# A new order of VectorE, GpSimd and ScalarE in the first stage of a two-layer transformer kernel, with x loaded ahead of the projection slices

## The chip, the cores and the metric

The kernel runs on one core of a Trainium2 chip. The metric is the time of one execution on the device, in microseconds. Of the kernel before there are three timed runs and one profiled execution.

## The reference

x is 2 x 256 rows of 512, the context 2 x 512 rows of 512. `layernorm` has no gain or bias. Four residual steps follow each other:

```python
# 1: both operands fake-quantised to 8 bits, (clip(round(v / s + z), 0, 255) - z) * s
x = x + fq(layernorm(x)) @ fq(ctx)                              # per batch, 512 x 512
# 2: a gated feed-forward, 512 -> 1376 -> 512; in blocks of 32 along the contraction the
#    rows are rounded to fp6 and the weights to fp4, with a shared power of two per block
x = x + mx_ffn(layernorm(x), w_gate, w_up, w_down)
# 3: cross attention: 32 query heads over 8 key and value heads of 128, rotary, masked softmax
x = x + attention(layernorm(x), ctx, wq, wk, wv, wo, mask)
# 4: a gated feed-forward with plain weights, 512 -> 1376 -> 512
x = x + ffn(layernorm(x), gate_w, up_w, down_w)
```

## The kernel before

Every engine has a list of instructions of its own (`@block.sync`, `tensor`, `scalar`, `gpsimd`, `vector`), written out by hand. An engine takes its list in order; what it has to wait for is a count of a semaphore. One wait at the head of a list holds all that is behind it.

**The first stage** does three things beside each other. TensorE projects the context to keys and values of step 3, in units of 128 x 512 results: `("v", i, h)` is context tile i with half h of the value heads, `("k", i, b)` key head i of batch b, and `("l", b, n)` one of the three products of step 1's attention for batch b. `STEPS` (L41) lists the units of eight steps; each takes the next of four PSUM banks in turn (`ROTATE`, L63, `take`, L515), and so waits until the unit four places back has been read (`drained`, L290). The first four value units are done together, slice by slice of the contraction (`first_values`, L550): slice k needs `slice_load(k)` (L337), a quarter of the context's columns and of the value weights, 512 KB. `keep_busy` (L544) issues `WARM` matmuls of ones before that. Five key units come later (`LATE_KEYS`, L51), between the products of step 2 and the first scores.

ScalarE copies each unit out (`copy_values`, `copy_keys`, L879 and L886), SyncE stores it to memory, and the keys of head 0 are loaded again for rotation (`first_keys_load`, L356, six loads into the place of weight buffers; it waits for 14 counts of `mx_free`, which are the halves of chunks 0 to 6).

The fp4 weights of step 2 come in 9 chunks of 128 x 2048 (the last is 128 x 512). A chunk i goes through `mx_peaks` (L1412, VectorE: block maxima), `mx_exponents` (L1418, VectorE, into one of `NRAW` = 3 slots), `scale_in` (L1146, GpSimd: multiply by the inverse scale, two halves), `mx_lift` (L893, ScalarE: magnitude to PSUM, two halves; half h of chunk i waits for `mx_free` 2(i-1)+h+1), `mx_round` (L1424, VectorE: two instructions a half, the second counts `mx_free`), `mx_clip` (L1437, VectorE), `scale_out` (L1155, GpSimd: multiply back, two halves), and `chunk_turn` (L345, SyncE: a transposing DMA into `WT`). VectorE's loop over chunks (L1467) puts the peaks and exponents of chunk i+2 behind the rounding of chunk i; GpSimd's (L1189) `scale_in(i+2)` ahead of `scale_out(i)`.

Step 1 is woven in. VectorE normalises x (`layernorm(True)`, L1383), ScalarE scales and rounds it (`rows_scale`, `rows_round`, L901 and L907), VectorE clips it (`clip_rows`, L1385), ScalarE makes the bf16 rows (`rows_keep`, L912), SyncE turns them (`rows_turn`). The context goes the same way (`context_scale`, `context_round`, `clip_context`, `context_keep`). With `L0_AT` = 4 the product's rank-one part is written by ScalarE (`share`, L927), GpSimd adds it to X (`rows_add`, L1181), and VectorE adds the product (`attention0`, L1401), behind the rounding of chunks 4 and 5. Behind chunk 5 VectorE also rounds chunk 6, then takes the second layer norm and quantises its rows to fp6 (L1487 to L1494); GpSimd scales them (`rows_out`, L1164), SyncE turns them (`rows_turn_again`, L364, two DMAs), and TensorE begins the gate and up products (`gate_up_slice`, L594), which wait for that, for chunks 0 to 5 and for key unit (5, 0). The late key unit in front of them (L629) waits for all of `mx_free` up to chunk 7.

**Between the stages** come the gate, up and down products of step 2, the third layer norm, and then the attention's units U = -3 to 64 in five parallel lists (`unit`, L456, L778, L1062, L1223, L1571). Unit U takes in a query head (rotary: ScalarE swaps halves into `q_swp`, GpSimd multiplies by the sine, L1235, VectorE by the cosine, L1602, and adds, L1615), and a pair of head and batch in four parts j: `score` (L695), the row maximum (L1587), the exponential (`exponent`, L1042), the division (L1230), the transposes (`turn_probs`), the weighing and the projection. `score` n waits for n - 1 exponentials (L703).

## Time and profile before

| what | value |
|---|---|
| median of three runs | 683.6 us (683.54 to 683.84) |
| the profiled execution, timed on the device | 683.66 us |
| its span, first to last instruction | 681.9 us |
| TensorE busy | 659.7 us (97%) |
| VectorE busy | 518.0 us (76%) |
| ScalarE busy | 344.7 us (51%) |
| GpSimd busy | 471.5 us (69%) |

The span is 1.8 us shorter than the execution's own time, which also holds what lies around it. A busy share is an average over stages: what a change in one of them is worth must be read from that stage. In the rows PE is TensorE, DVE VectorE, ACT ScalarE, POOL GpSimd, and SPq SyncE's queue of DMA issues. Times of rows are in us from the start of the span. A record of an instruction is longer than its distance to the next one, since instructions overlap by a part of their length.

### The profile page before, as it was taken

What the parts mean: (1) busy time and instruction counts of PE and PEld (TensorE: products, weight loads), DVE (VectorE), ACT (ScalarE), POOL (GpSimd) and SP (SyncE); (2) the same over time, 40 slices, a digit from 0 to 9 for tenths busy, and PEclk for the clock granted to TensorE, in tenths of its full rate; (3) what the DMA queues carried; (4) which work ended last, traced back from release to release, by engine and by line L of the source; (5) the groups of instructions that cost most, each with busy time, mean ns of one, the idle gap of its engine ahead of it and who ended that gap; (6) DMA issues with size and microseconds to landing.
All of it is one profiled execution on the core that took longest, in us unless ns stands there. A gap on an engine that the chain in (4) does not pass through costs nothing.

```text
span 681.9 us, 10810 instructions
## 1 busy us (share of the span) xinstructions
PE 659.7 (97%) x2993; PEld 484.8 (71%) x2996; DVE 518.0 (76%) x1024; ACT 344.7 (51%) x665; POOL 471.5 (69%) x435
## 2 busy tenths in 40 slices
PE   9998999899799999999999999999999999899998
PEld 3443444446567888888888888888888877788886
DVE  5999797997788888888888888888888886621113
ACT  1795223424656656656656656556656663221111
POOL 0688937337598688688788788698688477066661
PEclk9999999999999999999999999999999999999999
DMA  8999678403222222222222121222224012012321
GB/s 315 390 343 248 200 195 185 155 1 123 92 79 77 63 78 78 62 79 75 62 79 75 62 84 70 62 77 77 62 78 138 17 32 83 10 48 94 110 73 62
DMA packets 61260, 73.15 MB, mean 107 GB/s; under 512 B 25265, under 2 KB 33585, under 8 KB 60209
## 3 DMA queue, kind: packets, MB, share of 16 engines
q1 hardware_dynamic: 61232, 72.83, 34.7%
q8 instruction: 12, 0.20, 0.1%
q14 instruction: 16, 0.12, 0.1%
HBM read 58.00 MB, written 9.44 MB: 99 GB/s over the span
## 4 chain that ended last, share of the span: by engine, by line
PE 73%; DVE 12%; POOL 7%; issue 4%; ACT 2%; DMA 1%; SPq 0%; POOLq 0%; DVEq 0%; ACTq 0%
PE ps L687 16%; PE ps L689 16%; PE ps L688 16%; PE ps L755 11%; PE ps L721 7%; PE ps L572 3%; PE ps L540 2%; POOL mx_raw L1153 2%; PE ps L608 2%; POOL mx_w L1162 2%; DVE mx_amax L1416 1%; DVE stats L1329 1%; DVE xhat L1358 1%; POOL prob L1230 1%; DMA X<-in_x 1%
## 5 line engine op out<-in xcount | busy, mean ns | idle before, releaser
L1230 POOL TENSOR_SCALAR prob<-prob,rinv 128x512 f32<-128x512 f32 x128 | 89.4, 698 | 72.4 <-DVE rinv L1594 72.3
L1049 ACT ACTIVATE prob<-ps,nmax 128x512 f32<-128x512 f32 x128 | 88.3, 690 | 97.8 <-DVE nmax L1587 95.3
L755 PE MATMUL ps<-xt,wq_sb 128*128 128x512 f32 x384 | 103.1, 393 | 0.1
L1060 ACT CAST pT<-ps 128x512 fp32r<-128x512 f32 x128 | 75.1, 587 | 51.4 <-PE ps L721 50.4
L1587 DVE CUSTOM_DVE_ANT_0 ps<-ps,mask_sb 128x512 f32<-128x512 f32 x128 | 87.8, 686 | 5.1 <-PE ps L689 5.0
L1610 DVE TENSOR_TENSOR pT<-ps,pT 128x512 fp32r<-128x512 f32 x128 | 86.2, 674 | 3.0 <-ACT pT L1060 2.0
L755 PEld LDWEIGHTS ps<-xt,wq_sb 128*128 128x128 f32 x384 | 71.8, 188 | 17.2 <-issue 1.0
L721 PE MATMUL ps<-idf,prob 128*128 128x128 f32 x512 | 76.7, 272 | 0.4 <-POOL prob L1230 0.3
L721 PEld LDWEIGHTS ps<-idf,prob 128*128 128x128 f32 x512 | 63.8, 142 | 17.3 <-POOL prob L1230 1.6
L687 PE MATMUL ps<-pT,vt 128*128 128x512 f32 x128 | 61.2, 478 | 0.9 <-DVE pT L1610 0.9
L540 PE MATMUL ps<-ctxT,wk_sb 128*128 128x512 f32 x128 | 57.7, 594 | 0.0
L687 PE MATMUL ps<-kt,qt 128*128 128x512 f32 x128 | 50.8, 397 | 4.0 <-ACT prob L1049 3.5
L687 PE MATMUL ps<-wo_sb,oT 128*128 128x512 f32 x128 | 50.5, 394 | 2.0 <-DVE oT L1657 1.5
L1665 DVE SCALAR_TENSOR_TENSOR int<-ps,sc,silu 128x512 f32<-128x512 f32 x11 | 8.3, 750 | 57.6 <-PE ps L689 57.6
L1235 POOL TENSOR_TENSOR q_swp<-q_swp,ropeQ 128x512 f32<-128x512 f32 x32 | 47.5, 1484 | 6.1 <-ACT q_swp L1070 6.1
L689 PE MATMUL ps<-pT,vt 128*128 128x512 f32 x128 | 50.8, 397 | 0.0
L688 PE MATMUL ps<-pT,vt 128*128 128x512 f32 x128 | 50.3, 393 | 0.0
L1207 POOL TENSOR_TENSOR wo_sb<-wo_raw,wo_sb 128x512 fp32r<-128x512 f32 x32 | 48.4, 1512 | 2.7
L689 PE MATMUL ps<-kt,qt 128*128 128x512 f32 x128 | 50.1, 392 | 0.0
L688 PE MATMUL ps<-wo_sb,oT 128*128 128x512 f32 x128 | 50.0, 391 | 0.0
L689 PE MATMUL ps<-wo_sb,oT 128*128 128x512 f32 x128 | 50.0, 391 | 0.0
L688 PE MATMUL ps<-kt,qt 128*128 128x512 f32 x128 | 49.9, 390 | 0.0
(177 smaller groups left out, 1542.3 us busy)
## 6 DMA issues: line engine op xcount, KB each, us to landing
mx_raw<-in_mxw SPq DMA_DIRECT2D x8, 1024.0 KB, 6.9
wq_raw<-in_wq SPq DMA_DIRECT2D x32, 256.0 KB, 3.2
wo_raw<-in_wo SPq DMA_DIRECT2D x32, 256.0 KB, 2.6
v_scr<-v_st SPq DMA_DIRECT2D x16, 256.0 KB, 3.9
k_scr<-k_st SPq DMA_DIRECT2D x16, 256.0 KB, 3.4
kr<-k_scr SPq DMA_DIRECT2D x16, 256.0 KB, 2.8
kr_swp<-k_scr SPq DMA_DIRECT2D x32, 128.0 KB, 3.3
vr<-v_scr SPq DMA_DIRECT2D x16, 256.0 KB, 3.4
```

The costliest lines, as they stand in the source:

```text
L540: last = mm(bank(n), wk_sb[:, i % 2, k], ctxT[:, k, b * CTX:(b + 1) * CTX], start=(k == 0), stop=(k == KD - 1))
L687: mm(out_ap, left[0], right[0], start=first, stop=False)
L688: mm(out_ap, left[0], right[1], start=False, stop=False)
L689: return mm(out_ap, left[1], right[0], start=False, stop=final)
L721: last = nc.tensor.transpose(bank(2 + i % 2)[:, k * P:(k + 1) * P], prob[:, i, k * P:(k + 1) * P], idf[:])
L755: last = mm(query_bank(H), wq_sb[:, par, l, k], xt[:, r, k], start=(n == 0), stop=(n == 11))
L1049: nc.scalar.activation(prob[:, j], bank(j % 2), ACT.Exp, bias=nmax[:, j:j + 1], scale=-1.0, accum_out=rsum[:, j:j + 1]).then_inc(exps, 1)
L1060: copy(pT[:, v % 2, 0, :, i * P:(i + 1) * P], bank(2 + i % 2).rearrange("p (k c) -> p k c", k=4)).then_inc(ph_ready, 1)
L1207: tt(low, raw, high.bitcast(F32), ALU.subtract).then_inc(l_done, 1)
L1230: nc.gpsimd.tensor_scalar(prob[:, i], prob[:, i], rinv[:, i:i + 1], 1.0, ALU.mult, ALU.mult).then_inc(probs, 1)
L1587: nc.vector.tensor_tensor_reduce(out=bank(j % 2), in0=bank(j % 2), in1=mask_sb[:, 2 * (u % 2) + j % 2], scale=-1.0, scalar=BIG, op0=ALU.ad ...
L1610: tt(pT[:, v % 2, 1, :, i * P:(i + 1) * P], bank(2 + i % 2).rearrange("p (k c) -> p k c", k=4), pT[:, v % 2, 0, :, i * P:(i + 1) * P].bitc ...
```

## The change

- SyncE loads x's four row tiles first, then slice 0, weight chunk 0 and slices 1 to 3. Before, slices 0 and 1 came first, then x, slice 2, chunk 0, slice 3. All that follows stays as it was.
- `WARM` is 12 instead of 8.
- The exponents get a fourth slot (`NEXP`), so that VectorE's exponents of a chunk wait for one `scale_out` less.
- The clip of x's rows goes from VectorE (behind the peaks of chunk 2) to GpSimd (behind `scale_in(1)`).
- VectorE adds the first attention's products before GpSimd adds the rank-one part: `attention0` stands behind the exponents of chunks 5 and 6 (i = 3 and 4) and no longer waits for `l0_added`; `rows_add` waits for `l0_read` and stands ahead of `scale_in(6)` and `scale_in(7)`.
- The rounding of chunk 6 stands behind the second layer norm and the fp6 quantising, not ahead of them.
- ScalarE does `share(0)` ahead of `context_keep(1)`.
- SyncE's stores of k(4,1) and the units after it stand behind `chunk_turn(5)`, most of them behind the turning of the rows.
- At the start of the attention: the last late key unit is split over U = -2 and U = -1, GpSimd's sine for U = -2 goes between the two halves of a weight split, and the first row maximum and exponential are issued earlier.

The diff, cut to its core (the body of `row_max` is the old one, and `query_sine` is the old wait and multiplication in a function):

```diff
 NRAW = 3
+NEXP = 4
...
-WARM = 8
+WARM = 12
...
-            mx_e = sb("mx_e", [P, NRAW, CH // BLK], F32, a)
+            mx_e = sb("mx_e", [P, NEXP, CH // BLK], F32, a)
...
             sp.dma_start(sc[:], scalars).then_inc(sc_in, 16)
-            slice_load(0)
-            slice_load(1)
             for t in range(NT):
                 sp.dma_start(X[:, t], x[t * P:(t + 1) * P]).then_inc(x_in[t], 16)
+            slice_load(0)
+            mx_load(0)
+            slice_load(1)
             slice_load(2)
-            mx_load(0)
             slice_load(3)
...
             first_keys_load()
-            stores(STEPS[5][1] + STEPS[6][0])
             chunk_turn(5)
-            stores(STEPS[6][1])
+            stores(STEPS[5][1] + STEPS[6][0][:1])
             rows_turn_again(0)
             rows_turn_again(1)
-            stores(STEPS[7][0])
+            stores(STEPS[6][0][1:] + STEPS[6][1] + STEPS[7][0])
...
-                    if isinstance(U, int) and U == -1 and j == 3:
-                        late_keys(4, range(1, 4))
+                    if isinstance(U, int) and U in (-2, -1) and j == 3:
+                        late_keys(4, range(1, 2) if U == -2 else range(2, 4))
...
             copy_keys(2, 1)
+            share(0)
             context_keep(1)
-            share(0)
...
                 for j in range(4):
+                    if isinstance(U, int) and U == 0 and j == 0:
+                        exponent(0, 0, 0)
...
-                    exponent(U, u, j)
+                    if not (isinstance(U, int) and U == 0 and j == 0):
+                        exponent(U, u, j)
...
                     pool.wait_ge(l0_shared, t + 1)
+                    pool.wait_ge(l0_read, t + 1)
                     tt(X[:, t], X[:, t], xhat[:, t], ALU.add).then_inc(l0_added, 1)

             scale_in(0)
             scale_in(1)
+            pool.wait_ge(q1_rounded, 1)
+            rows = xhat[:].rearrange("p t d -> p (t d)")
+            ts(rows, rows, ROUND, ROUND + 255.0, ALU.max, ALU.min).then_inc(q1_clipped, 1)

             for i in range(NFULL):
+                if i in (L0_AT, L0_AT + 1):
+                    rows_add(i - L0_AT)
                 if i + 2 <= NFULL:
                     scale_in(i + 2)
-                if i in (L0_AT - 1, L0_AT):
-                    rows_add(i - L0_AT + 1)
                 scale_out(i)
...
-            def split(high, low, raw, h_done, l_done, count):
+            def split(high, low, raw, h_done, l_done, count, between=None):
                 pool.sem_inc(pool_past_wait, 1)
                 nc.gpsimd.tensor_scalar(high, raw, 1.0, 1.0, ALU.mult, ALU.mult).then_inc(h_done, 1)
+                if between:
+                    between()
                 pool.wait_ge(h_done, count)
                 tt(low, raw, high.bitcast(F32), ALU.subtract).then_inc(l_done, 1)
...
-                    if isinstance(U, int) and U in (-2, -1) and j == 0:
-                        query_split(U, u, g)
-                    if j == 0 and within(U + 2, NH):
-                        pool.wait_ge(q_swapped, U + 3)
-                        tt(q_swp[:].rearrange("p (b c) -> p b c", b=BATCH), q_swp[:].rearrange("p (b c) -> p b c", b=BATCH),
+                    if isinstance(U, int) and U == -2 and j == 0:
+                        query_split(U, u, g, lambda: query_sine(-2))
+                    elif j == 0 and within(U + 2, NH):
+                        if isinstance(U, int) and U == -1:
+                            query_split(U, u, g)
+                        query_sine(U)
...
-            def clip_rows():
...
                     dve.wait_ge(l0_sums, 2 * b + t % 2 + b + 2)
-                    dve.wait_ge(l0_added, t + 1)
                     stt(X[:, t], bank(rotating(("l", b, t % 2 + 1))), sx[:, 4:5], X[:, t], ALU.mult, ALU.add).then_inc(l0_read, 1)
...
-                after(dve, mx_ready, 2 * (i - NRAW + 1))
+                after(dve, mx_ready, 2 * (i - NEXP + 1))
...
             for i in range(NFULL):
-                if i != L0_AT + 2:
-                    mx_round(i, 0)
-                    mx_round(i, 1)
+                mx_round(i, 0)
+                mx_round(i, 1)
                 if i + 2 <= NFULL:
                     mx_peaks(i + 2)
-                if i in (L0_AT, L0_AT + 1):
-                    attention0(i - L0_AT)
-                if i == 0:
-                    clip_rows()
...
                 mx_clip(i)
                 if i + 2 <= NFULL:
                     mx_exponents(i + 2)
+                if i in (L0_AT - 1, L0_AT):
+                    attention0(i - L0_AT + 1)
                 if i == L0_AT + 1:
-                    mx_round(i + 1, 0)
-                    mx_round(i + 1, 1)
-                    dve.wait_ge(l0_read, NT)
+                    dve.wait_ge(l0_added, NT)
                     layernorm(False)
...
-                    if within(U, NUNIT):
...
+                    if within(U, NUNIT) and not (isinstance(U, int) and U == 0 and j == 0):
+                        row_max(U, u, j)
...
                         tt(q_cos[:], q_cos[:], q_swp[:], ALU.add).then_inc(q_roped, 1)
+                    if isinstance(U, int) and U == -1 and j == 2:
+                        row_max(0, 0, 0)
```

## Rows read from the trace of the kernel before

**Rows 1.** Busy time by stretch: us; busy (instructions) per engine, clock, DMA share, GB/s

```profile
0.00:111.00 111.00, 104.56 (x251) 44.63 (x253) 98.11 (x132) 54.58 (x67) 70.08 (x51) 1.00 0.90 273
...
200.00:570.00 370.00, 368.64 (x1849) 304.23 (x1848) 313.63 (x684) 229.52 (x495) 294.17 (x291) 1.00 0.23 70
```

**Rows 2.** Timeline of TensorE: start, duration, line, tiles, count [idle before <-releaser]

```profile
1.01 3.59 PE L548 MATMUL ps<-ones 128*128 128x512 bf16 x8 [1.01 <-POOL ones L1138]
4.93 14.25 PE L558 MATMUL ps<-wv_sb,ctxT 128*128 128x512 f32 x32 [0.32 <-DMA wv_sb<-in_wv]
...
26.83 7.11 PE L572 MATMUL ps<-wv_sb,ctxT 128*128 128x512 f32 x16 [0.79 <-DMA wv_sb<-in_wv]
...
78.12 7.13 PE L572 MATMUL ps<-wv_sb,ctxT 128*128 128x512 f32 x16 [1.36 <-DVE X L1406]
...
111.04 9.96 PE L608 MATMUL ps<-WT,q1T 128*128 128x512 bf16 x48
```

**Rows 3.** Timeline of VectorE, the first weight chunks

```profile
22.04 1.21 DVE L1432 SCALAR_TENSOR_TENSOR mx_raw<-ps,mx_raw 128x1024 f32<-128x1024 bf16 x1
...
29.00 1.22 DVE L1387 TENSOR_SCALAR xhat<-xhat 128x2048 f32<-128x2048 f32 x1
...
30.84 1.22 DVE L1432 SCALAR_TENSOR_TENSOR mx_raw<-ps,mx_raw 128x1024 f32<-128x1024 bf16 x1
```

**Rows 4.** Timeline of GpSimd, 59 to 105 us

```profile
59.45 0.24 POOL L1149 TENSOR_SCALAR mx_r<-mx_e 128x64 int32<-128x64 int32 x1 [1.88 <-DVE mx_e L1422]
...
70.52 0.24 POOL L1149 TENSOR_SCALAR mx_r<-mx_e 128x64 int32<-128x64 int32 x1 [0.32 <-DVE mx_e L1422]
...
85.65 3.78 POOL L1162 TENSOR_TENSOR mx_w<-mx_q,mx_e 128x1024 bf16<-128x1024 bf16 x2
100.07 4.23 POOL L1168 TENSOR_TENSOR q<-f6c,f_e 128x1024 bf16<-128x1024 bf16 x2 [10.63 <-DVE f6c L1460]
```

**Rows 5.** Timeline of VectorE, second layer norm and fp6

```profile
86.19 2.46 DVE L1329 BATCH_NORM_STATS2 stats<-X 128x6 f32<-128x512 f32 x4
...
89.10 0.36 DVE L1344 TENSOR_SCALAR var_eps<-meanvar 128x4 f32<-128x4 f32 x1
...
99.90 0.68 DVE L1416 TENSOR_REDUCE mx_amax<-mx_raw 128x16 f32<-128x512 f32 x1
...
102.45 1.88 DVE L1422 TENSOR_SCALAR mx_e<-mx_amax 128x16 uint32<-128x16 uint32 x1
```

**Rows 6.** Timeline of ScalarE, 89 to 93 us

```profile
89.21 1.98 ACT L899 ACTIVATE ps<-mx_raw 128x1024 f32<-128x1024 f32 x2
92.16 0.59 ACT L884 COPY k_st<-ps 128x512 f32<-128x512 f32 x1 [0.97 <-PE ps L540]
```

**Rows 7.** Timeline of SyncE's issues; last, median us from issue at 103.56 to landing

```profile
92.12 0.63 SPq L360 DMA_DIRECT2D kr<-k_scr  x1
...
100.06 2.76 SPq L349 DMA_TRANSPOSE WT<-mx_w  x1
...
103.56 3.03 SPq L367 DMA_TRANSPOSE q1T<-q  x2
...
q1T<-q SPq DMA_TRANSPOSE x1, 4.0
```

**Rows 8.** SyncE's issues of x and chunk 0, and from issue to landing of each

```profile
3.09 1.85 SPq L374 DMA_DIRECT2D X<-in_x  x4
...
DMA to landing us min/median/max: 5.1/5.4/5.7
...
6.10 0.71 SPq L312 DMA_DIRECT2D mx_raw<-in_mxw  x1
...
mx_raw<-in_mxw SPq DMA_DIRECT2D x1, 1024.0 KB, 7.9
```

**Rows 9.** Timelines of ScalarE and TensorE at the first scores

```profile
175.02 0.69 ACT L1049 ACTIVATE prob<-ps,nmax 128x512 f32<-128x512 f32 x1
...
175.95 0.47 PE L687 MATMUL ps<-kt,qt 128*128 128x512 f32 x1 [1.91 <-ACT prob L1049]
```

More of the change, by code:

```diff
@@ L1148, in scale_in @@
                 pool.wait_ge(mx_expo, i + 1)
-                ts(mx_r[:, p, 0:m].bitcast(I32), mx_e[:, p, 0:m].bitcast(I32), -1.0, -(2.0 ** 24), ALU.mult, ALU.add).then_inc(mx_scale, 1)
+                ts(mx_r[:, p, 0:m].bitcast(I32), mx_e[:, i % NEXP, 0:m].bitcast(I32), -1.0, -(2.0 ** 24), ALU.mult, ALU.add).then_inc(mx_scale, 1)
                 pool.wait_ge(mx_scale, i + 1)
@@ L1158, in scale_out @@
                     pool.wait_ge(WT_in[i - 2], 16)
-                p, e = i % 2, i % NRAW
+                p, e = i % 2, i % NEXP
                 for cols in halves(i):
@@ L1214, in _, with query_sine, query_split @@
             split(wq_sb[:, 0, 0], wq_sb[:, 0, 1], wq_raw[:, 0], wqh_ready, wq_split, 1)
-            def query_split(U, u, g):
+            def query_sine(U):
+                pool.wait_ge(q_swapped, U + 3)
+                tt(q_swp[:].rearrange("p (b c) -> p b c", b=BATCH), q_swp[:].rearrange("p (b c) -> p b c", b=BATCH),
+                   ropeQ[:, 1].unsqueeze(1).to_broadcast([P, BATCH, SEQ]), ALU.mult).then_inc(q_sined, 1)
+            def query_split(U, u, g, between=None):
                 H, par = U + 4, u % 2
@@ L1220, in query_split @@
                     after(pool, q_sums, H - 1)
-                    split(wq_sb[:, par, 0], wq_sb[:, par, 1], wq_raw[:, par], wqh_ready, wq_split, H + 1)
+                    split(wq_sb[:, par, 0], wq_sb[:, par, 1], wq_raw[:, par], wqh_ready, wq_split, H + 1, between)
             def unit(U, u, g):
@@ L1383, in quantise_rows @@
                 layernorm(True)
-            def clip_rows():
-                dve.wait_ge(q1_rounded, 1)
-                ts(rows(xhat[:]), rows(xhat[:]), ROUND, ROUND + 255.0, ALU.max, ALU.min).then_inc(q1_clipped, 1)
             def clip_context(b):
@@ L1418, in mx_exponents @@
             def mx_exponents(i):
-                p, m = i % NRAW, width(i) // BLK
-                after(dve, mx_ready, 2 * (i - NRAW + 1))
+                p, m = i % NEXP, width(i) // BLK
+                after(dve, mx_ready, 2 * (i - NEXP + 1))
                 dve.wait_ge(mx_peak, i + 1)
@@ L1569, in _, with row_max @@
             dve.wait_ge(mask_in, 16)
+            def row_max(U, u, j):
+                n = 4 * U + j
+                dve.wait_ge(scores, n + 1)
+                dve.sem_inc(dve_past_wait, 1)
+                nc.vector.tensor_tensor_reduce(out=bank(j % 2), in0=bank(j % 2), in1=mask_sb[:, 2 * (u % 2) + j % 2],
+                                               scale=-1.0, scalar=BIG, op0=ALU.add, op1=ALU.min,
+                                               accum_out=nmax[:, j:j + 1]).then_inc(rowmax, 1)
             def unit(U, u, g):
@@ L1581, in unit @@
                         tt(oT[:, u % 2, 1], bank(4 + u % 2), oT[:, u % 2, 0].bitcast(F32), ALU.subtract).then_inc(o_split, 1)
-                    if within(U, NUNIT):
-                        n = 4 * U + j
-                        dve.wait_ge(scores, n + 1)
-                        dve.sem_inc(dve_past_wait, 1)
-                        nc.vector.tensor_tensor_reduce(out=bank(j % 2), in0=bank(j % 2), in1=mask_sb[:, 2 * (u % 2) + j % 2],
-                                                       scale=-1.0, scalar=BIG, op0=ALU.add, op1=ALU.min,
-                                                       accum_out=nmax[:, j:j + 1]).then_inc(rowmax, 1)
+                    if within(U, NUNIT) and not (isinstance(U, int) and U == 0 and j == 0):
+                        row_max(U, u, j)
                     V, v, i = (U, u, j - 1) if j else (U - 1, (u - 1) % 4, 3)
```

1 line of the change is left out of this document (removed).

## The prediction

> **What bounds the kernel now.** I read the busy time by stretch first. From 200 to 570 us TensorE is busy 368.64 of 370.00 us, so a shift of its work ahead of that passes to the end one for one, and what matters is when the first stage lets go. There, up to 111 us, TensorE has 104.56 us of work and VectorE 98.11: neither has much slack [rows 1]. TensorE's timeline then shows its projections, in records 0.43 us apart, starting at 4.93 and reaching the gate and up products of the first feed-forward at 111.04 without a wait. On the way it stood still for a load (0.79 us) and three times for the first attention's banks, 1.50, 1.36 and, in the row shown, 1.36 [rows 2].
>
> VectorE rounds weight chunk 0 from 22.04, in four instructions of 1.2 us like the one shown, so 4.8 us a chunk, and chunk 1 from 30.84; the rows' clip stands between them [rows 3]. GpSimd runs from 59.45 to 89.43, stopping only twice for 0.32 us, one of them shown; its end there is 85.65 + 3.78 [rows 4]. VectorE begins the second layer norm at 86.19. The four-wide operation at 89.10 lasts 0.36, to 89.46, the end of GpSimd's work, and the layer norm and its fp6 quantising are over at 99.90 [rows 5]. At 102.45 a small operation that needs 0.2 us takes 1.88 and ends at 104.33, with GpSimd's pair of 100.07 to 104.30 [rows 4, 5]. So GpSimd holds VectorE's operations of these kinds for a whole instruction.
>
> ScalarE lifts chunk 7 at 89.21 and copies k(4,1) at 92.16 [rows 6]. SyncE issues the first keys' six loads from 92.12, about 0.62 us each, the transpose of chunk 5 at 100.06 and the rows' two at 103.56; the first of those two lands 4.0 us later, at 107.6, in time for 111.04 [rows 7].
>
> **The start.** x now goes first, slice 0 second, chunk 0 third. The queue lands in order, so I read places off by megabytes. The second row tile was the bytes up to 1.5 MB: issued near 3.56, landed at 8.8; the fourth (2.0 MB) 4.52 + 5.7 = 10.2; chunk 0 (3.5 MB) 6.10 + 7.9 = 14.0 [rows 8]. Now slice 0 ends at 1.5 MB, 8.8; slice 1 at 3.0 MB, about 12.7; the later two by 14.0 and 15.3. A slice is eight records, 3.4 us: 8.9 to 12.3, a 0.5 us wait, 12.8 to 23.1. Before, this pass ended at 19.0: +4.1. The 0.79 us wait at 26.83 is then past: +3.3 [rows 2].
>
> Twelve warm matmuls instead of eight cost 4 x 0.45 = 1.8 us at most and end near 6.4, in front of 8.8: nothing.
>
> The layer norm of x is over some 3 us earlier, but ScalarE copies v(0,0) and v(1,0) ahead of lift 0, and they wait for the late pass. Unit 0 is summed at 20.9, unit 1 at 21.7; a copy (0.6) and a lift (1.0) [rows 6] give rounding at 23.4 instead of 22.04: +1.3. GpSimd takes the rows' clip off VectorE, -1.1 [rows 3]: chunk 1 is rounded at +0.2. GpSimd does it between scale_in(1) and scale_in(2), which waits for chunk 2's exponents until 31; at most it costs twice its nearest row's 1.9 us for 1024 columns of two inputs, 3.8 [rows 4], at least VectorE's 1.2, and I take 2.5. Either fits behind rows_round at 26.2. Were it not to fit, one or two us of rows_keep would be late, which nothing needs before the rows' first transpose.
>
> **The middle.** The copies, lifts and context steps in ScalarE's queue move by up to 3 us with TensorE, still ahead of their readers. Sharing before context_keep(1) frees the bank for v(4,1) in time. TensorE, 3.3 late, finds the attention's banks drained: its waits (4.2) go, so by itself it would reach 111.04 at 110.1, -0.9. On VectorE attention0 goes behind exponents and in front of rounding 4 and 5; rows_add waits for l0_read, and VectorE no longer for l0_added. The fourth exponent slot removes two waits of VectorE for scale_out. GpSimd is the chain here: from 59.7 it has the same instructions, with its adds in front of the scaling, and so ends again at about 89.5 [rows 4].
>
> The second layer norm no longer has rounding of chunk 6 in front of it: it can start at 86.2 - 4.8 + 0.3 = 81.7. It then runs beside scale_in(7) and scale_out(5). Statistics pass. The first small operation, at 84.6, waits to about 85.9, the next to 87.8, the next to 89.7. The other eight steps (0.2 each) and the normalising (1.9) come after, so the layer norm ends where it did, and fp6 at about 100.0 [rows 5]. That stall of about 4.6 us is what cancels the early start. The Trainium skill (SBUF — State Buffer, section SBUF: two separate sides) calls the shared pair an exclusive lock for a whole instruction, taken by any VectorE operation with two SBUF inputs too. No row shows the tiny two-input ones; with the rule the sum is mine, without it that of the second rival.
>
> **What hangs on chunk 6.** Its rounding is now behind fp6: 100.0 to 104.8, where it ended at 86.19. Three queues wait for it.
> - SyncE: first_keys_load waits for mx_free 14, that rounding, and all behind it waits too. 104.8 + 3.7 (six loads) + 2.8 (chunk 5) + 1.1 (two stores) = 112.4, the issue of the rows' transpose; + 4.0 = 116.4 [rows 7]. Moving two stores behind it saves about 1.1 and is in this sum.
> - ScalarE: lift(7,0) and lift(7,1) wait for the same, and k(4,1)'s copy is behind them: 104.8 + 1.0 + 0.6 = 106.4 [rows 6].
> - TensorE: v(7,1) needs k(4,1)'s bank. It is idle from 100.5 to 106.4, then has 3.4 + 3.4 + 1.7 (v(7,1), k(5,0), half a late key) = 115.0. The late key's wait for chunk 7's rounding, 110.8, is inside.
>
> So the gate product starts at 116.4 instead of 111.04: +5.4. From there to 200 us chains of VectorE and TensorE follow one another from that product on, and shift with it.
>
> **The late edits.** k(7,1)'s four matmuls are the same work at two places; the sine between the halves of one split comes 1.3 us earlier, but TensorE is busy without a gap up to 174.0, the first score included, so that buys nothing. The first maximum and exponential go ahead of q_swp. TensorE waited 1.91 at 175.95 for that exponential; at best this goes. But q_swp is now behind the exponential's 0.9 us, and the next maximum is behind q_swp on VectorE: at worst +0.9 [rows 9]. Score 3, which needs the second exponential, then waits instead. I take 0, since the wait moves by one score.
>
> **Sum.** -0.9 never shows, +5.4 replaces it. The profiled execution took 683.66 (span 681.9); 683.66 + 5.4 = 689.06. It is 0.06 above the median 683.6, so 689.0.
>
> **Rivals.**
> - The clock falls (15%). The eight bf16 matmuls at the start took 0.45 us each, the 1.2 GHz level, against 0.21 in the 48 at 111.04, 2.4 GHz; the granted column reads 1.00 at both. TensorE had been idle before the eight [rows 2]. No pause over 1.91 us is in the rows used. If 5.9 us idle drops it, some 3.6 us run at half pace and 1.8 are lost: 115.0 becomes 116.8, the forecast +0.4, 689.4. If the pause from 6.4 to 8.9 does too, the head of every queue is 1.8 late: 691.2. The Trainium skill (TensorE: Matmul & The Clock Gate, Part 1) has the clock return to half after idling; by that rule the first of these is likely.
> - Only some small operations are held (15%). Two are (89.10 and its like), the two-input ones not: fp6 ends near 98.2, everything 1.8 less: 687.2.
> - None is held (10%). 81.7 + 13.7 = 95.4, 4.6 less: +0.8, 684.4. Against it speak 0.36 at 89.10 and 1.88 at 102.45.
> - Not slower (18%): chunk 6 is done in time. SyncE needs 11.6 us from its rounding to the landing, so from an end at 99.4 downward nothing is lost, and at 98.5 TensorE's own 110.1 rules. It takes free small operations and x's order costing no 1.3 us. Then -0.9, 682.7; with the late wait of 1.91 gone too, 680.8. For it: the rows' order does bring x 3 us forward, and two waits of VectorE go.
> - The forecast has the other 42%.
>
> The measurement can tell about 0.2%, 1.4 us. Faster than 682.2 is 12% (the fourth rival with the late gain), within is 13% (its rest and part of the third), slower 75%. The range: 682.6 takes in most of the fourth, 691.5 the clock twice; outside are some 12% below and 5% above.
>
> **What would show it.** Right: first values at 8.9 and out of the last slice near 23; rounding 0 at 23.4; layer norm starting near 81.7 with small operations of 1 to 2 us; chunk 6 rounded after 104; SyncE's key loads after that; TensorE idle some 6 us before its last value product; the gate product at 116. Wrong: fp6 over by 96, key loads before 100, the gate product before 111, or a gap of 1.9 us at the scores that simply goes.

## The result and the profile after

The changed kernel takes 695.05 us in the median of four runs (693.14 to 695.89), the kernel before 683.72 (683.54 to 684.21): a ratio of 1.0161, with a 95% interval from 1.0138 to 1.0184. That is 11.3 us slower. The forecast was 689.0, slower by 5.4, and 691.5 was the top of its range: the direction was right, the size wrong by 6 us.

| what | before | after |
|---|---|---|
| profiled execution | 683.66 us | 695.89 us |
| its span | 681.9 us | 694.0 us |
| TensorE busy | 659.7 us | 666.7 us |
| VectorE busy | 518.0 us | 525.3 us |
| start of the gate product | 111.04 us | 121.25 us |

The span grew by 12.1 us, of which 10.2 lie ahead of the gate product. This is busy time by stretch in the changed kernel: us; busy (instructions) of TensorE, its weight loads, VectorE, ScalarE and GpSimd; granted clock; DMA share; GB/s.

```profile
0.00:111.00 111.00, 99.98 (x238) 43.24 (x239) 98.16 (x125) 51.78 (x63) 73.42 (x51) 0.96 0.81 246
8.60:24.00 15.40, 15.39 (x32) 6.76 (x33) 7.91 (x15) 4.08 (x4) 7.47 (x6) 0.89 1.03 399
...
109.50:116.00 6.50, 6.46 (x8) 2.71 (x9) 4.33 (x4) 1.45 (x3) 4.79 (x3) 0.53 1.01 231
...
200.00:570.00 370.00, 367.83 (x1837) 302.60 (x1837) 314.74 (x685) 231.47 (x497) 294.58 (x288) 1.00 0.22 71
```

Against [rows 1] the late stretch is as full as it was. In the first 111 us TensorE has less work done, and its granted clock is no longer 1.00: it is 0.89 over the first values and 0.53, all but the lower level of 1.2 GHz, from 109.5 to 116. TensorE's timeline shows the same, beside [rows 2]:

```profile
0.99 5.30 PE L548 MATMUL ps<-ones 128*128 128x512 bf16 x12 [0.99 <-POOL ones L1141]
8.61 15.67 PE L558 MATMUL ps<-wv_sb,ctxT 128*128 128x512 f32 x32 [2.31 <-DMA wv_sb<-in_wv]
...
91.71 10.46 PE L572 MATMUL ps<-wv_sb,ctxT 128*128 128x512 f32 x24
109.54 6.72 PE L572 MATMUL ps<-wv_sb,ctxT 128*128 128x512 f32 x8 [7.37 <-ACT k_st L884]
116.09 5.31 PE L540 MATMUL ps<-ctxT,wk_sb 128*128 128x512 f32 x12
121.25 9.96 PE L608 MATMUL ps<-WT,q1T 128*128 128x512 bf16 x48
```

The 24 value matmuls at 91.71 take 10.46 us, 0.43 each. The eight of the same kind at 109.54, behind a pause of 7.37 us, take 6.72, twice as long each. The waits for the first attention's banks, 4.2 us before, are gone, as forecast, and nothing came of it.

VectorE's timeline, beside [rows 3] and [rows 5]:

```profile
24.14 1.23 DVE L1441 SCALAR_TENSOR_TENSOR mx_raw<-ps,mx_raw 128x1024 f32<-128x1024 bf16 x1 [3.76 <-ACT ps L899]
...
31.13 3.55 DVE L1449 TENSOR_SCALAR mx_q<-mx_q 128x2048 bf16<-128x2048 bf16 x1
...
34.69 1.21 DVE L1441 SCALAR_TENSOR_TENSOR mx_raw<-ps,mx_raw 128x1024 f32<-128x1024 bf16 x1
...
84.99 2.48 DVE L1343 BATCH_NORM_STATS2 stats<-X 128x6 f32<-128x512 f32 x4
87.50 0.38 DVE L1349 BATCH_NORM_AGGREGATE meanvar<-stats 128x2 f32<-128x6 f32 x4
87.92 1.31 DVE L1358 TENSOR_SCALAR var_eps<-meanvar 128x4 f32<-128x4 f32 x1
89.26 1.83 DVE L1361 TENSOR_SCALAR rstd<-var_eps 128x4 int32<-128x4 int32 x1
91.13 1.83 DVE L1368 SCALAR_TENSOR_TENSOR newton<-rstd 128x4 f32<-128x4 f32 x1
92.99 0.16 DVE L1369 TENSOR_TENSOR newton<-newton,var_eps 128x4 f32<-128x4 f32 x1
...
102.99 1.22 DVE L1441 SCALAR_TENSOR_TENSOR mx_raw<-ps,mx_raw 128x1024 f32<-128x1024 bf16 x1
```

Chunk 0 is rounded from 24.14, 2.1 us later than before; chunk 1 from 34.69, 3.85 later. Between them stands a clip of chunk 0 that takes 3.55 us instead of 0.69. From there the delay is carried: layer norm at 84.99, then exactly three small operations held (1.31, 1.83, 1.83, against 0.16 for the next; GpSimd works without a stop from 85.42 to 92.94, and the third ends at 92.96), fp6 over and chunk 6's rounding begun at 102.99. What held the clip stands in GpSimd's timeline, the one instruction that moved there:

```profile
27.06 7.07 POOL L1194 TENSOR_SCALAR xhat<-xhat 128x2048 f32<-128x2048 f32 x1 [2.47 <-ACT xhat L910]
```

It runs to 34.13, and the clip of chunk 0 ends 0.55 us behind it. On ScalarE's queue the lift of chunk 7 waits for chunk 6's rounding, 16.49 us up to 105.56 for its first half, and the copy that TensorE's last value product waits for stands behind the second half, at 108.91:

```profile
108.91 0.58 ACT L884 COPY k_st<-ps 128x512 f32<-128x512 f32 x1
```

The same rounding holds SyncE's queue, beside [rows 7]; the rows' transpose lands 4.3 us after its issue, at 120.3:

```profile
107.88 0.34 SPq L361 DMA_DIRECT2D kr<-k_scr  x1
...
111.29 3.46 SPq L350 DMA_TRANSPOSE WT<-mx_w  x1
114.80 0.58 SPq L323 DMA_DIRECT2D k_scr<-k_st  x1
115.43 0.42 SPq L328 DMA_DIRECT2D v_scr<-v_st  x1
115.96 2.87 SPq L368 DMA_TRANSPOSE q1T<-q  x2
```

Behind the gate product another 1.9 us are lost. TensorE's timeline at the first scores, beside [rows 9], and GpSimd's:

```profile
178.29 3.02 PE L755 MATMUL ps<-xt,wq_sb 128*128 128x512 f32 x12 [0.74 <-POOL wq_sb L1216]
185.63 0.47 PE L687 MATMUL ps<-kt,qt 128*128 128x512 f32 x1 [0.28 <-ACT prob L1049]
188.94 0.50 PE L687 MATMUL ps<-kt,qt 128*128 128x512 f32 x1 [1.46 <-ACT prob L1049]
```

```profile
175.28 1.29 POOL L1227 TENSOR_TENSOR q_swp<-q_swp,ropeQ 128x512 f32<-128x512 f32 x1 [0.49 <-ACT q_swp L1072]
176.52 1.72 POOL L1216 TENSOR_TENSOR wq_sb<-wq_raw,wq_sb 128x512 fp32r<-128x512 f32 x1
```

The wait of 1.91 us shrank to 0.28, but 1.46 follows at the next score, and the split's low half now comes behind the sine, so that TensorE waits 0.74 for it. In the kernel before the low half starts 0.70 us after the start of its high half (163.92), here 2.35 after it (174.17). GpSimd's timeline before:

```profile
164.62 1.29 POOL L1207 TENSOR_TENSOR wq_sb<-wq_raw,wq_sb 128x512 fp32r<-128x512 f32 x1
```

### The profile page after: what moved, and what is told of

Read it like the earlier page. It is cut to its first block, busy times and chain, and to the rows that moved or that the text cites. A ratio compares the mean times of both kernels' runs of the same rounds, so it can differ in the third digit from the quotient of the medians.

```text
span 694.0 us, 10820 instructions
## 1 busy us (share of the span) xinstructions
PE 666.7 (96%) x3000; PEld 487.2 (70%) x3000; DVE 525.3 (76%) x1023; ACT 345.5 (50%) x665; POOL 479.6 (69%) x436
## 4 chain that ended last, share of the span: by engine, by line
PE 66%; DVE 19%; issue 7%; POOL 4%; ACT 3%; DMA 1%; SPq 0%; DVEq 0%; ACTq 0%; POOLq 0%
PE ps L687 14%; PE ps L689 14%; PE ps L688 14%; PE ps L755 10%; PE ps L721 6%; DVE mx_raw L1441 2%; PE ps L558 2%; PE ps L608 2%; DVE mx_amax L1425 2%; PE ps L540 2%; DVE ps L1579 1%; PE ps L572 1%; DVE stats L1343 1%; DVE xhat L1372 1%; DVE mx_q L1449 1%
## 5 line engine op out<-in xcount | busy, mean ns | idle before, releaser
L687 PE MATMUL ps<-kt,qt 128*128 128x512 f32 x128 | 51.0, 399 | 3.3 <-ACT prob L1049 2.7
L572 PE MATMUL ps<-wv_sb,ctxT 128*128 128x512 f32 x96 | 45.5, 627 | 7.4 <-ACT k_st L884 7.4
L689 PE MATMUL ps<-kt,qt 128*128 128x512 f32 x128 | 50.2, 392 | 0.0
```

The costliest lines, as they stand in the source:

```text
L572: last = mm(bank(n), ctxT[:, k, i * P:(i + 1) * P], wv_sb[:, k, h * 512:(h + 1) * 512], start=(k == 0), stop=(k == KD - 1))
L687: mm(out_ap, left[0], right[0], start=first, stop=False)
L689: return mm(out_ap, left[1], right[0], start=False, stop=final)
```

## The experiments

The theory after reading the trace: the chain that was forecast (layer norm held, chunk 6 late, SyncE's queue) is right, and GpSimd's clip, TensorE's clock and the late edits add what is missing. The rivals: the clip fits and costs nothing; the loads are what costs; the pace of TensorE has nothing to do with its pauses; the late edits are free.

### The rows' clip back on VectorE

```diff
-            pool.wait_ge(q1_rounded, 1)
-            ts(rows, rows, ROUND, ROUND + 255.0, ALU.max, ALU.min)
...
+                if i == 0:
+                    clip_rows()
```

> The changed kernel, with one part undone: the rows' clip is on VectorE again, behind the peaks of chunk 2, instead of on GpSimd. Theory (the clip takes GpSimd 7.07 us, keeps scale_in(2) and so VectorE's clip of chunk 0 waiting, and makes rounding of chunk 1 start at 34.69 us): VectorE's 3.55 us clip of chunk 0 goes back to about 0.6, the rows' clip costs about 1.1, rounding of chunk 1 starts near 33, and the gate product and the end come about 1.7 us earlier, 693.4 us, ratio to the kernel before 1.014. Rival (the clip fits beside other work, as predicted): rounding of chunk 1 may move, the gate product stays at 121.3 and the time at 695.1, 1.0165.

693.62 us, 1.0151 (1.0133 to 1.0169). VectorE's timeline:

```profile
30.96 1.22 DVE L1398 TENSOR_SCALAR xhat<-xhat 128x2048 f32<-128x2048 f32 x1
32.09 0.69 DVE L1450 TENSOR_SCALAR mx_q<-mx_q 128x2048 bf16<-128x2048 bf16 x1
...
32.80 1.22 DVE L1442 SCALAR_TENSOR_TENSOR mx_raw<-ps,mx_raw 128x1024 f32<-128x1024 bf16 x1
```

Chunk 0's clip takes 0.69 again and chunk 1 is rounded 1.9 us earlier. The medians differ by 1.4 us where 1.7 was expected, and the intervals of the two kernels overlap, so that the time alone does not decide. The trace shows the hold gone. In this profiled execution the gate product even starts 3.1 us earlier, at 118.15; 1.2 of that is its last value product, which took 5.53 us instead of 6.72.

### A product in place of the clip

```diff
-            ts(rows, rows, ROUND, ROUND + 255.0, ALU.max, ALU.min)
+            ts(rows, rows, 1.0, 1.0, ALU.mult, ALU.mult)
```

> The changed kernel, with GpSimd's 2048-column instruction a product by 1.0 and 1.0 instead of a maximum and a minimum, so x's rows are not clipped; same operands, same place, same waits. Theory (it is the kind of operation that is dear: GpSimd's products by two constants take 0.6 to 0.7 us for 512 columns): this one takes 2.4 to 2.8 us instead of 7.07, VectorE's clip of chunk 0 is not held beyond 1.3 us, rounding of chunk 1 starts near 32 instead of 34.69, time about 692.0 to 692.5 us, ratio 1.012 to 1.013. Rival (any one-input instruction over 2048 float32 columns takes 7 us on GpSimd, 3.45 ns a column): 7.07 us, 34.7, 695.

The rows are not clipped in this kernel. 690.47 us, 1.0111 (1.0089 to 1.0133). GpSimd's timeline, then VectorE's:

```profile
25.41 1.90 POOL L1194 TENSOR_SCALAR xhat<-xhat 128x2048 f32<-128x2048 f32 x1 [1.31 <-ACT xhat L910]
```

```profile
29.48 0.68 DVE L1449 TENSOR_SCALAR mx_q<-mx_q 128x2048 bf16<-128x2048 bf16 x1
...
30.18 1.22 DVE L1441 SCALAR_TENSOR_TENSOR mx_raw<-ps,mx_raw 128x1024 f32<-128x1024 bf16 x1
```

The same bytes in the same place cost 1.90 us as a product and 7.07 as a maximum and a minimum. So it is the kind of operation, and the rival with 3.45 ns for every one-input column falls; which of the two, the maximum or the minimum, is dear was not separated. The Trainium skill (GPSIMD Engine Reference, 4.1 Engine selection) calls GpSimd roughly line-rate for one input; the product agrees, 0.93 ns a column, the maximum and minimum do not, 3.45 ns. The gain is 4.6 us by the medians, 3.4 by the ratios, where 2.5 to 3 was expected. In the trace the hold of 2.9 us is gone; another part is TensorE's clock, which did not fall at the start of this profiled execution: chunk 0 is rounded at 22.50 instead of 24.14. Runs at the same mean granted clock tell the two apart: three of this kernel at 0.995 took 690.1 to 690.6, the one run of the changed kernel at 0.995 took 693.14, 2.8 us more; this kernel's fourth, at 0.989, took 693.4 against 695.6 and 695.89 of the changed kernel at 0.990. So the clip is worth some 2.2 to 2.8 us, from one run or two on each side. In this profiled execution the gate product starts at 115.58 where the prediction had 116.4, so the clip and the clock at the start make up all of the first stage's miss. The last value product still took 5.56 us there, behind a pause of 5.13.

### Chunk 6 rounded ahead of the layer norm again

```diff
                 if i == L0_AT + 1:
+                    mx_round(i + 1, 0)
+                    mx_round(i + 1, 1)
                     dve.wait_ge(l0_added, NT)
```

> The changed kernel, with one part undone: chunk 6 is rounded ahead of the second layer norm and its fp6 again, as before the change; the order of rows_add and l0_read stays the new one. Theory (the layer norm gains nothing from its early start, and the rounding put behind it holds up SyncE's key loads, ScalarE's lifts and TensorE's last value product): the layer norm ends at about the same time, near 103 to 104; the key loads go out near 92 instead of 105; TensorE has no pause of 7 us before its last value product and shows no stretch at half the granted clock there; the gate product starts near 114.5 instead of 121.3; time about 688.3 us, ratio 1.0067. Rival (the layer norm's early start is worth what the late rounding costs): gate product at 119 or later, time 693 or more, ratio 1.0135 or more.

689.46 us, 1.0092 (1.0069 to 1.0115), 5.6 us under the changed kernel by the medians, 4.7 by the ratios. TensorE's timeline:

```profile
110.89 2.41 PE L540 MATMUL ps<-ctxT,wk_sb 128*128 128x512 f32 x4 [3.70 <-DVE mx_q L1444]
113.09 11.23 PE L608 MATMUL ps<-WT,q1T 128*128 128x512 bf16 x48
```

Its fp6 is over at 101.55. This profiled execution runs 1.8 us ahead from the start, since the clock did not fall there; without that lead the changed kernel's 102.99 would be 101.15. So 4.8 us of rounding ahead of the layer norm delay its end by 0.4: its early start was worth almost nothing, and the rival falls. SyncE loads the keys at 89.91 instead of 107.88, and the pause of 7.37 us before the last value product is gone. One of 3.70 us takes its place, for chunk 7's rounding, and the gate product behind it takes 11.23 us instead of 9.96: the clock again.

### The old loads

```diff
-WARM = 12
+WARM = 8
...
+            slice_load(0)
+            slice_load(1)
             for t in range(NT):
                 sp.dma_start(X[:, t], x[t * P:(t + 1) * P]).then_inc(x_in[t], 16)
```

> The changed kernel, with one part undone: the old order of the first loads (slices 0 and 1, x, slice 2, chunk 0, slice 3, chunk 1) and eight instead of twelve warm matmuls. Theory (GpSimd's long clip, 26 to 33 us, rules the start whatever the loads do): the first values start near 5, TensorE is ahead of the others by up to 4 us more and gives that back before its last value product; rounding of chunk 1 starts near 34.0 instead of 34.69; time about 0.7 us less, 694.4, ratio 1.0155. Rival (the late loads are the cost: 3.3 us on TensorE and 1.3 on VectorE): 691 to 692 us, ratio 1.011 to 1.012.

694.22 us, 1.015 (1.0133 to 1.0167). Chunk 0 is rounded at 21.71, 2.4 us earlier, but chunk 1 at 33.59, only 1.1 earlier: GpSimd's clip runs from 25.95 to 33.02 and takes the rest. The time is 0.8 us less, within the intervals, and the rival, loads as the main cost, falls for this kernel, where the clip hides what they cost.

### TensorE kept busy in the pause

```diff
-                for k in range(KD):
+                for _ in range(3 if (i, h) == (7, 0) else 1):
+                    for k in range(KD):
```

> The changed kernel, with the first half-width value product of the last row tile (24 us of the first stage's end) computed three times instead of once, so that TensorE works through most of its pause ahead of the last value product; 16 matmuls are extra work, the output is the same. Theory (the 7.4 us of idling halve the pace of the following 8 matmuls): these take 0.43 us each instead of 0.85, 3.4 us in all instead of 6.7; the gate product is then set by the transpose of the rows, which lands near 120.2, so it starts at 120.0 to 120.3 instead of 121.3; time about 1.1 us less, 694.0, ratio 1.015. Rival (idling isn't what halves the pace): the eight matmuls still take 6.7 us, and the time is the same or up to 3 us more.

TensorE's timeline:

```profile
109.98 3.70 PE L573 MATMUL ps<-wv_sb,ctxT 128*128 128x512 f32 x8 [0.52 <-ACT k_st L885]
...
120.43 9.95 PE L609 MATMUL ps<-WT,q1T 128*128 128x512 bf16 x48 [1.60 <-DMA q1T<-q]
```

The eight matmuls take 3.70 us instead of 6.72, with the pause down to 0.52, so the pause was the cause of their pace. The gate product now waits 1.60 us for the rows' transpose, as expected. The time did not fall, though: 695.97 us, 1.0169 (1.0148 to 1.019). The start was 0.4 us later in the profiled execution, and of the 0.8 us won at the gate product nothing is left 39 us later: TensorE then waits 0.33, 1.15 and 0.90 us for VectorE between the gated slices, where it waited 0.56 and 1.15. The time of this run was missed by 2 us.

Then the same with SyncE's key loads behind the rows' transposes:

```diff
-            first_keys_load()
             chunk_turn(5)
...
             rows_turn_again(1)
+            first_keys_load()
```

> The changed kernel with v(7,0) computed three times, and SyncE's six key loads moved behind the rows' transposes. Theory (with TensorE kept at the full clock, the gate product waited 1.60 us for the transpose of the rows, and this stood behind the key loads, which wait for chunk 6's late rounding): the transposes go out near 105.5 instead of 116 us, land by 110, the wait of 1.60 us goes, and the gate product starts near 118.8 instead of 120.4, on TensorE's own work; time 694.0 to 694.4, ratio 1.0145 to 1.015. Rival (another wait stands right behind): gate product at 120 or later, 695.5 or more.

693.75 us, 1.0147 (1.0129 to 1.0165), an interval that overlaps the changed kernel's, and in TensorE's timeline no wait at the gate product:

```profile
109.68 3.70 PE L573 MATMUL ps<-wv_sb,ctxT 128*128 128x512 f32 x8 [0.20 <-ACT k_st L885]
...
118.37 9.95 PE L609 MATMUL ps<-WT,q1T 128*128 128x512 bf16 x48
```

So two chains met at the gate product within a microsecond: SyncE's, through the key loads, and TensorE's, through the half-paced product. Either alone hides the other: the gate product came 0.8 us earlier with the first step and 2.9 with both.

### Warm matmuls up to the first slice

```diff
-WARM = 12
+WARM = 24
```

> The changed kernel with 24 warm matmuls at the start instead of 12, so that TensorE works up to the landing of slice 0. Theory (the pause of 2.3 us behind the warm matmuls makes the first value product run at half pace for about 3.4 us, in some executions and not in others, which costs the head of every queue 1.6 us and spreads the times over 2.7 us): the 32 value matmuls all stand 0.43 us apart and end near 22.3 instead of 24.1 us, rounding of chunk 0 starts near 22.5, the time is 693.3 us with a spread under 1 us, ratio 1.0138. Rival (the pause is no cause): as the changed kernel, 693.1 to 695.9, median 695.

693.94 us, 1.0141 (1.0126 to 1.0157), spread 1.2 us. TensorE's timeline:

```profile
8.41 3.67 PE L558 MATMUL ps<-wv_sb,ctxT 128*128 128x512 f32 x8 [0.25 <-DMA wv_sb<-in_wv]
12.51 10.54 PE L558 MATMUL ps<-wv_sb,ctxT 128*128 128x512 f32 x24 [0.42 <-DMA wv_sb<-in_wv]
```

All 32 stand 0.43 us apart, and chunk 1 is rounded at 33.46 instead of 34.69. The median gains 1.1 us of the 1.7 expected; the intervals overlap, and it is the trace that shows the cause.

### The late edits, together and apart

The first run puts all of them on the kernel before, as the change's diff has them.

> The kernel before, with the late edits alone: the first maximum and exponential ahead of the sum for the second query, the sine between the two halves of one weight split, k(7,1)'s four matmuls at two places. The first stage is that of before. Theory (the wait of 1.91 us comes back as other waits, and the split's low half is late for TensorE): from the gate product to the first score 61.2 instead of 60.15 us, from there to the end 511.5 instead of 510.7; time 683.8 + 1.9 = 685.7 us, ratio 1.0028. Rival (worth nothing, as predicted): 683.8 us, within 0.3.

685.2 us, 1.0018 (1.0009 to 1.0027), and 1.0 us more from gate product to end. The next two take GpSimd's edit alone and the first maximum and exponential alone.

```diff
+                        query_split(U, u, g, lambda: query_sine(-2))
```

```diff
+                    if isinstance(U, int) and U == -1 and j == 2:
+                        row_max(0, 0, 0)
...
+                    if isinstance(U, int) and U == 0 and j == 0:
+                        exponent(0, 0, 0)
```

> The kernel before, with GpSimd's late edit alone: the sine product between the high and the low half of one query weight's split. Theory: the low half is ready 1.7 us later, TensorE waits about 0.7 us for it in front of the twelve matmuls at 178 us of the changed kernel, and the first score is as much later; time 683.8 + 0.7 = 684.5 us, ratio 1.001. Rival 1: all of the 1.07 us ahead of the first score come from it, 684.9. Rival 2: the sine's early end gives the wait back by the scores, 683.8.

> The kernel before, with one late edit alone: VectorE's first maximum and ScalarE's first exponential ahead of the steps for the second query; the sine and k(7,1) as before. Theory (the late edits cost 1.1 us together, and the sine's place nothing, so the maximum's place costs it): the wait of 1.91 us for the exponential shrinks to 0.3, and waits of 1.5, 0.5 and 0.3 us follow that the kernel before has not; time about 1.1 us over the kernel before, 685.0 us, ratio 1.0016. Rival (the split of k(7,1)'s matmuls is what costs): same as before, 683.9 us.

683.53 us, 0.9995 (0.9986 to 1.0004), for the sine; 684.25 us, 1.0003 (0.9994 to 1.0012), for the maximum. Both theories were wrong, and with them the idea that one edit holds the cost: each alone is free. That left the pair, or k(7,1), for one more run, the two diffs together.

> The kernel before with two late edits, the sine between the halves of the split and the first maximum and exponential ahead of the second query's steps, but k(7,1)'s matmuls as before. Each of the two alone cost nothing (0.9995 and 1.0003), the two and the split of k(7,1) together 1.0018. Theory (the late low half is hidden as long as TensorE waits 1.9 us for the exponential later anyway; take that wait away and it shows): TensorE waits 1.6 us for the low half near 168 us, the wait for the exponential is 0.3, and waits of 1.45, 0.5 and 0.3 follow; time 1.1 to 1.9 us over the kernel before, ratio 1.0016 to 1.0028. Rival (the split of k(7,1) alone is what costs): 684.0 us, 1.000.

685.53 us, 1.0027 (1.0017 to 1.0038). The pair costs 1.9 us without k(7,1). TensorE's timeline with the sine alone:

```profile
167.85 3.03 PE L755 MATMUL ps<-xt,wq_sb 128*128 128x512 f32 x12 [1.60 <-POOL wq_sb L1209]
176.04 0.47 PE L687 MATMUL ps<-kt,qt 128*128 128x512 f32 x1 [0.30 <-ACT prob L1049]
```

With the maximum alone:

```profile
174.31 0.47 PE L687 MATMUL ps<-kt,qt 128*128 128x512 f32 x1 [0.30 <-ACT prob L1049]
177.61 0.50 PE L687 MATMUL ps<-kt,qt 128*128 128x512 f32 x1 [1.45 <-ACT prob L1049]
```

With both:

```profile
168.01 3.02 PE L755 MATMUL ps<-xt,wq_sb 128*128 128x512 f32 x12 [1.59 <-POOL wq_sb L1212]
176.20 0.47 PE L687 MATMUL ps<-kt,qt 128*128 128x512 f32 x1 [0.30 <-ACT prob L1049]
179.51 0.50 PE L687 MATMUL ps<-kt,qt 128*128 128x512 f32 x1 [1.46 <-ACT prob L1049]
```

With the sine alone, the wait of 1.6 us for the low half only takes the place of the 1.91 us which TensorE would spend waiting for the exponential. With the maximum alone, the score comes 1.6 us earlier and gives that back in waits of 1.45, 0.50 and 0.27, where the kernel before had one of 0.91. With both, the early wait is there and nothing later swallows it. With two of k(7,1)'s six matmuls in front (prediction and expectations speak of four), as in the change, the wait for the low half is 0.74 instead of 1.59; whether that saves time the intervals (1.0018 and 1.0027) don't settle.

### All that was sized wrongly, taken out

The changed kernel with the late edits undone and

```diff
+WARM = 24
...
+                for _ in range(3 if (i, h) == (7, 0) else 1):
...
+            ts(rows, rows, 1.0, 1.0, ALU.mult, ALU.mult)
```

> The changed kernel with everything taken out that the prediction had sized wrongly, and nothing else: GpSimd's instruction on the rows is a product by 1.0 (1.9 us instead of 7.07; the rows are not clipped), 24 warm matmuls and v(7,0) three times keep TensorE's clock up, the late edits are undone. The order of VectorE, GpSimd, ScalarE and SyncE in the first stage, and the loads, are those of the change. Theory (the prediction's chain through the layer norm, chunk 6's late rounding and SyncE was right, and these four terms are the whole miss): rounding of chunk 1 near 30.7, fp6 over at 99.0, chunk 6 rounded by 103.8, the rows' transpose landed and the gate product started at 116.3 us, time 689.0 us, ratio 1.0075. Rival 1 (a term is still missing in the chain): 690.5 or more. Rival 2 (the terms overlap, so that less is left than predicted): 687.5 or less.

689.99 us, 1.0094 (1.0079 to 1.011); its profiled execution 689.48. VectorE's, SyncE's and TensorE's timelines:

```profile
98.70 1.22 DVE L1432 SCALAR_TENSOR_TENSOR mx_raw<-ps,mx_raw 128x1024 f32<-128x1024 bf16 x1
```

```profile
111.42 2.89 SPq L368 DMA_TRANSPOSE q1T<-q  x2
```

```profile
115.76 9.95 PE L609 MATMUL ps<-WT,q1T 128*128 128x512 bf16 x48 [0.23 <-DMA q1T<-q]
```

Every step of the chain is within 0.6 us of what was expected, and the gate product starts at 115.76 where the prediction had 116.4, released by the rows' transpose. The time is 1 us over 689.0, and the ratio expected of this run, 1.0075, lies just under the interval, so something under 1 us is still missing; in the profiled execution 0.7 us of it lie behind the gate product, 571.5 us to the end against 570.9 before.

### A version that beats both

The kernel before with four exponent slots, the new order of the first attention and of SyncE's stores, nothing of the rest, and chunk 7 rounded straight behind the fp6:

```diff
                     fp6_clip(NT * D, [])
+                    mx_round(i + 2, 0)
+                    mx_round(i + 2, 1)
```

> A version that may beat both: the kernel before with four exponent slots, the new order of the first attention (behind VectorE's exponents, GpSimd's adds in front of its scaling, share ahead of context_keep) and of SyncE's late stores; the rows' clip on VectorE, the old loads, chunk 6 rounded ahead of the second layer norm, none of the late edits; and chunk 7 rounded straight behind the layer norm's fp6, ahead of the peaks of chunk 8 and the clip of chunk 6. Theory (the late key product waits for chunk 7's rounding, which these two small operations and their holds by GpSimd, 4.3 us in all, now put off; the waits for the attention's banks, 4.2 us, are gone): rounding of chunk 7 ends near 104.7 instead of 109.0, TensorE reaches the gate product at 107.0 to 108.0 instead of 111.04, the rows' transpose lands near 107.6; time about 680.5 us, ratio 0.995. Rival 1 (the rows' transpose lands later than in the kernel before, as behind the moved stores): gate product near 110, 682.7, ratio 0.9985. Rival 2 (chunk 8 and the weights' transposes behind it are late for the products after the gate): no gain, 683.8.

682.21 us, 0.9978 (0.9969 to 0.9987): 1.7 us under the kernel before, 12.8 under the changed one. TensorE's timeline:

```profile
108.29 3.61 PE L608 MATMUL ps<-WT,q1T 128*128 128x512 bf16 x16 [1.66 <-ACT k_st L884]
112.85 8.31 PE L608 MATMUL ps<-WT,q1T 128*128 128x384 bf16 x40 [0.95 <-DVE int L1511]
```

The gate product starts 2.75 us earlier than before, and 1.1 of it is given back in the slices behind. Which of the edits brings how much was not separated. Two steps more, ScalarE's copy of k(5,0) ahead of the lift of chunk 8 and chunk 8 rounded between two products of VectorE, were meant to fetch that.

```diff
+            copy_keys(5, 0)
             mx_lift(NFULL, 0)
-            copy_keys(5, 0)
...
             inter_product(0, 0)
+            mx_round(NFULL, 0)
+            mx_clip(NFULL)
             inter_product(0, 1)
```

> The version that beat the kernel before by 1.7 us, with two steps more: ScalarE copies k(5,0) ahead of the lift of chunk 8, and VectorE rounds chunk 8 between the first two products of the gated slices instead of in front of them. Theory (there the gate product waited 1.66 us for that copy, and the second gate slice 0.95 us for VectorE, which stood 2.48 us at chunk 8's second rounding): gate product at 107.0 to 107.6 instead of 108.29, no wait of 0.95 us; time about 680.4 us, ratio 0.995. Rival (the rows' transpose or chunk 8's late clip take the gain back): 682.2, ratio 0.9975.

682.41 us, 0.9975 (0.9966 to 0.9984). The gate product starts at 107.16, 1.1 us earlier again, and TensorE then waits 0.45 and 1.61 us for VectorE: the rival was right.

## Why the prediction was right or wrong, point by point

- **The start.** First values were forecast at 8.9 and came at 8.61; chunk 0's rounding at 23.4 and came at 24.14. The clock more than makes up the 0.7 us between: at full pace chunk 0 starts at 22.3 to 22.9, as four other profiled executions show, so the new loads cost 0.3 to 0.9 us there and not the 1.3 of the forecast.
- **The rows' clip, which failed.** The step took 2.5 us, bounded by 1.2 and "twice its nearest row's 1.9 us for 1024 columns of two inputs, 3.8", and said "Either fits". It took 7.07. The nearest row by columns was a product, and no row of the kernel before showed GpSimd take a maximum or a minimum. With 3.8 us it would have ended at 30.9, ahead of VectorE's clip at 31.13. At 34.13 it held that clip for 2.9 us, and chunk 1 came at 34.69 instead of 31.0. The prediction also looked for the damage in the wrong place, in `rows_keep`, and not at VectorE's next operation that GpSimd can hold, the bf16 clip of chunk 0. Measured price: some 2.2 to 2.8 us.
- **The waits for the attention's banks** (4.2 us) went, as said.
- **The layer norm** was right in mechanism, to the instruction: three small operations held, one of them with two inputs, which [rows 5] had not shown, and by the amount forecast (4.5 us in all, 4.6 forecast). All of it lay 3.0 us later, from the clip and the start. The two rivals with fewer held operations fall, and the Trainium skill's rule for two inputs (SBUF — State Buffer, SBUF: two separate sides) is borne out by the 1.83 us at 91.13.
- **Chunk 6 behind fp6** was right. From the end of that rounding SyncE's queue needed 12.5 us to the landing, 11.6 forecast. Putting the rounding back gains 5.6 us by the medians, 4.7 by the ratios, part of it the clock, which did not fall at the start of that profiled execution.
- **The clock, left out of the sum,** was a rival at 15%, with 0.4 us, or 2.2 if it fell twice. It fell twice. The last value product took 3.0 us more (6.72 against 3.70 at full pace), not the 1.8 forecast: it ran almost wholly at half pace. Together with the 3 us of the clip this put TensorE's own path to 121.25, behind SyncE's at 120.3. The mechanism was named and its chance was too low. The row that should have weighed more was the one at 4.93 [rows 2]: full pace there came behind eight half-paced matmuls and a pause of 0.32, while the change made both pauses long. The Trainium skill (TensorE: Matmul & The Clock Gate, Part 1) says that idling brings the clock down; the runs agree, 6.72 us for the eight matmuls behind 7.37 us of idling and 3.70 with most of it filled.
- **The late edits** were taken at 0, from 1.9 us faster to 0.9 slower. They cost 1.2. The step said of the sine that it "buys nothing", and did not count what stands behind it in GpSimd's queue: the low half, which starts 1.7 us later behind its high half (2.35 us instead of 0.70). It is free only under the wait of 1.91, which another edit takes away. Two edits were priced apart that share one cover.
- **The sum.** Taking the four mis-sized terms out (the clip, the clock at either pause, the late edits) leaves a kernel at 1.0094, against 1.0079 forecast (689.0 to 683.6), the lower end of its interval. The whole of the change measures 11.3 us: 6.4 in that kernel, 2.8 for the clip, 1.1 for the clock at the start, 1.2 for the late edits, 11.5 in all. That it closes so well is in part luck: the clip is read at the upper of its two values, and the intervals of these runs are 0.6 to 1.6 us to either side. The half-paced last value product appears in none of these on its own, since SyncE's chain ends within 1 us of it.

Between its waits at 227.96 and 592.69 us, with none over 0.3 us between them, the profiled execution of the changed kernel took 0.4 us longer than that of before took for the same work, and 0.7 longer than that of the same late code with the key loads behind. The second difference can't come from the late code; its cause is open.

## What to carry to other kernels

Price an instruction moved to another engine by a row of that engine with the same operation; where there is none, the range has to be wide, and the question is which instruction of the neighbour it will hold. Two edits that each cost nothing can cost together, when both hide under the same wait: sum the covers, not only the costs. A long pause on TensorE can cost more than its own length. Here pauses of 2.3 us and more were followed by work at half pace, which cost another 1.6 to 3.0 us, and pauses up to 1.95 us were not; a chain that ends in a long pause should be priced with such a loss behind it.

## What the runs showed of the hardware

- GpSimd took 7.07 us for a maximum and a minimum with constants over 2048 float32 columns, in each of six profiled executions, and 1.90 us for a product by two constants over the same columns in both that had it.
- TensorE at the start: after the warm matmuls and a pause of 2.31, 2.45, 2.74 and 2.79 us in four kernels, part of the first values ran at half pace; after 1.77, 1.95 and 0.25 us in three others none did. In the changed kernel the weight loads there stand 0.43 us apart up to 9.5, 0.85 from 10.1 to 12.7, and 0.43 again from 13.4: the fall came behind the pause, inside running work. The changed kernel's times spread over 2.7 us with this, and its four runs are ordered by their mean granted clock: 0.995 at 693.14, 0.993 at 694.5, 0.990 at 695.6 and 695.89.
- Behind the pause of 3.70 us ahead of the late keys the four key matmuls took 2.41 us instead of 1.88, and the gate product behind them 11.23 instead of 9.96. Behind pauses of 5.13, 6.24, 7.05, 7.17 and 7.37 us ahead of the last value product its eight matmuls took 5.56, 5.53, 6.74, 6.47 and 6.72 us, against 3.70 at full pace.
